# A layer of convolution by scan and a 4-bit feed-forward: statistics in sets of groups 0 to 3 and 4 to 7, the first x wholly through GpSimd, last banks opened by ScalarE, and new orders

## The reference

```
xn  = (x - mean) / sqrt(var + 1e-5)                    # over the last axis
out = x + conv(xn) + ffn(xn)

conv: a causal convolution along the sequence with the complex filter
      init * phazor^t, phazor = exp((angle*1j - exp(l)) * scale),
      plus last_conv * phazor^(t+1); times the gate 1 - exp(-exp(l)*scale); the real part
ffn:  q(v) = each block of 16 along the last axis divided by max|.|/6, rounded to the
      grid 0, .5, 1, 1.5, 2, 3, 4, 6 with its sign, and multiplied back
      gate = q(xn) @ q(w_gate).T;  up = q(xn) @ q(w_up).T           # 352 wide
      h = silu(gate) * up;         ffn = q(h) @ q(w_down).T         # 128 wide
```

## Time and profile before

| | |
|---|---|
| median of 3 runs | 121.2 us (119.83 to 121.43) |
| profiled execution | 120.77 us |
| its span, first to last instruction | 118.7 us |
| busy PE, DVE, ACT, POOL | 109.0, 101.6, 105.4, 100.3 us |
| granted TensorE clock | 1.00 |
| moved by DMA | 4.90 MB |

### The profile page before, as it was taken

How to read it: one execution, slowest core, us unless ns; L and a number is a source line. 1 busy time by engine, 2 the same in 40 slices (tenths; PEclk the granted TensorE clock), 3 DMA queues, 4 the chain that set the end, 5 groups by cost and what they waited for, 6 DMA issues and landing times.

```text
span 118.7 us, 2355 instructions
## 1 busy us (share of the span) xinstructions
PE 109.0 (92%) x661; PEld 83.6 (70%) x661; DVE 101.6 (86%) x219; ACT 105.4 (89%) x229; POOL 100.3 (85%) x119
## 2 busy tenths in 40 slices
PE   0599799989699999999999999999999999999992
PEld 0599455355357577877788876787788878879891
DVE  0798899999999999999899999898998699998300
ACT  4798889999999998999999999898989899898640
POOL 4578887991999999999999899999899999999400
DMA  3992000000000000020002000200020020020202
GB/s 98 340 359 104 0 3 0 3 3 6 0 0 0 0 0 0 0 94 0 0 3 94 0 3 0 88 0 6 0 88 0 0 88 0 6 91 0 88 22 66
DMA packets 3323, 4.90 MB, mean 41 GB/s; under 512 B 496, under 2 KB 1392, under 8 KB 3312
## 3 DMA queue, kind: packets, MB, share of 16 engines
q1 hardware_dynamic: 3168, 4.77, 11.6%
q10 hardware_dynamic: 144, 0.00, 0.1%
HBM read 2.67 MB, written 2.10 MB: 40 GB/s over the span
## 4 chain that ended last, share of the span: by engine, by line
PE 69%; ACT 12%; DVE 5%; issue 2%; ACTq 0%; DVEq 0%
PE ps_o L1305 16%; PE ps_u L1250 14%; PE ps_g L1231 14%; PE ps_h L1269 8%; PE ps_u L1257 6%; ACT xn L805 3%; PE ps_o L1294 3%; PE ps_x L1216 2%; PE ps_x L1202 2%; ACT silu L849 2%; ACT sqh L862 1%; ACT xsq L813 1%; DVE ps_u L1724 1%; DVE ps_u L1691 1%; ACT xq_T L842 1%
## 5 line engine op out<-in xcount | busy, mean ns | idle before, releaser
L1231 PE MATMUL ps_g<-wg_T,xq_T 128*128 128x352 f32 x64 | 25.0, 472 | 0.6 <-ACT silu L849 0.2
L1305 PEld LDWEIGHTS ps_o<-wd_T,hq_T 128*128 128x128 f32 x174 | 22.2, 192 | 2.1
L1305 PE MATMUL ps_o<-wd_T,hq_T 128*128 128x128 f32 x174 | 23.6, 275 | 0.0
L1250 PE MATMUL ps_u<-wu_T,xq_T 128*128 128x352 f32 x64 | 22.6, 466 | 0.2 <-DVE hq L1732 0.2
L855 ACT COPY hq_T<-ps_h 128x384 f32<-128x384 f32 x32 | 15.3, 479 | 2.8 <-PE ps_h L1269 2.8
L1685 DVE TENSOR_TENSOR ps_u<-silu,ps_u 128x704 f32<-128x704 f32 (+1 forms) x17 | 14.4, 844 | 2.2 <-PE ps_u L1250 2.1
L1269 PE MATMUL ps_h<-ident,hq 128*128 128x128 f32 x96 | 15.9, 274 | 0.3 <-ACT wd_T L782 0.2
L849 ACT ACTIVATE silu<-ps_g 128x352 f32<-128x352 f32 x32 | 14.9, 464 | 1.0 <-PE ps_g L1231 0.9
L1269 PEld LDWEIGHTS ps_h<-ident,hq 128*128 128x128 f32 x96 | 11.7, 142 | 5.1 <-issue 3.7
L1691 DVE TENSOR_REDUCE ps_u<-ps_u 128x44 f32<-128x704 f32 (+1 forms) x17 | 14.3, 849 | 0.2
L1724 DVE TENSOR_TENSOR ps_u<-ps_u,inv 128x704 f32<-128x704 f32 (+1 forms) x17 | 14.3, 845 | 0.2
(11 more groups left out here) (171 smaller groups left out, 246.1 us busy)
## 6 DMA issues: line engine op xcount, KB each, us to landing
x_all<-x_in SPq DMA_DIRECT2D x8, 256.0 KB, 4.6
out<-x_all SPq DMA_DIRECT2D x7, 256.0 KB, 2.0
w_raw<-w_in SPq DMA_DIRECT2D x2, 192.0 KB, 3.4
out<-x_all SPq DMA_DIRECT2D x4, 64.0 KB, 1.6
w_raw<-w_in SPq DMA_DIRECT2D x1, 176.0 KB, 3.6
par<-params_in ACTq DMA_DIRECT2D x1, 3.5 KB, 3.0
```

The source lines that it names most:

```text
L1231: pe.matmul(ps_g[:, 0:I], x_cols(t), wg_T[:, :], start=True, stop=True).then_inc(s_gate, 1)
L1250: pe.matmul(slot(q)[:, j, 0:I], x_cols(t), wu_T[:, :], start=True, stop=True).then_inc(s_up, 1)
L1305: m = pe.matmul(out_cols(t), hq_T[t % NHT][:, c * P:(c + 1) * P], wd_T[:, c, :], start=False, stop=(c == NCH - 1), skip_group_check=True)
```

## The change

The statistics now come in a set of groups 0 to 3 and a set of groups 4 to 7; the temporaries of the second lie in pair 3's slot, so its first step waits for up tile 7. Groups 2 and 3 are normalised from the first set. With `XH = 0`, both halves of group 0 go through `divide_x`, `square_x`, `big_x`, `shift_x`, `shift_back_x` and `scale_x`; `divide_first`, `square_first`, `round_first` and `scale_first` have no calls any more. A new step `open_last` (ACT) copies x of the last three tiles into their banks, and `sum_parts` waits for it in place of its own matmuls. Pair 9 instead of pair 12 is scaled on POOL. The first warm-up has 29 products instead of 21. And the four lists have new orders; SP's list of DMAs is the same. The definitions of `whole_turns` and `out_table` are only moved in the text.

```
-    STAT = ((0, 2), (2, 8))
-    STAT_SLOT = (0, 1)
-    XH = 1
+    STAT = ((0, 4), (4, 8))
+    STAT_SLOT = (0, 3)
+    XH = 0
-    BY_POOL = (11, 12, 13)
+    BY_POOL = (9, 11, 13)
...
+        s_openl = sem("x_in_last_banks")
...
-            return (ps_o[:, 0:D], slot(LAST - 1)[:, 0, 0:D], ps_x[:, 0:D], ps_g[:, 0:D])[t - (NT - TG)]
+            return (ps_o[:, 0:D], slot(LAST - 1)[:, 0, 0:D], ps_x[:, GT - D:GT], ps_g[:, 0:D])[t - (NT - TG)]
...
+            def open_last(t):
+                if t == NT - 3:
+                    slot_read(act, LAST - 1)
+                elif t == NT - 2:
+                    act.wait_ge(s_xnTc, NG)
+                else:
+                    act.wait_ge(s_silu, NT)
+                act.copy(last_bank(t), x_all[:, t, :]).then_inc(s_openl, 1)
...
                 else:
-                    if t == NT - 3:
-                        slot_read(pe, LAST - 1)
-                    elif t == NT - 2:
-                        pe.wait_ge(s_xnTc, NG)
-                    else:
-                        pe.wait_ge(s_silu, NT)
-                    pe.matmul(out_cols(t), ident[:, :], x_all[:, t, :], start=True, stop=True)
+                    pe.wait_ge(s_openl, t - (NT - TG))
```

More of the change, by code:

```diff
@@ L953, in _ @@
-            normalise(3, 1)
-            normalise(3, 2)
-            silu_tile(5)
-            normalise(3, 3)
-            square_h(1)
-            square_x(2, 1)
-            big_h(1)
-            big_x(2, 1)
-            copy_weight(2)
+            normalise(3, 3)
+            square_x(2, 1)
+            copy_xqT(1, 1)
+            big_x(2, 1)
+            square_h(1)
+            silu_tile(4)
+            big_h(1)
+            copy_in_table(1)
+            silu_tile(5)
+            out_table(0)
@@ L974, in _ @@
-            normalise(4, 1)
-            silu_tile(8)
-            big_x(3, 1)
-            normalise(4, 2)
-            copy_hT(2)
-            silu_tile(9)
-            normalise(4, 3)
-            copy_xnT(1)
-            square_h(3)
+            silu_tile(10)
+            copy_hT(2)
+            copy_xnT(1)
+            normalise(4, 0)
+            normalise(4, 1)
+            normalise(4, 2)
+            square_h(3)
+            normalise(4, 3)
+            big_h(3)
+            turn_part(0, 0)
@@ L1032, in _ @@
             big_h(7)
-            copy_xqT(5, 1)
-            copy_hT(10)
+            copy_hT(12)
+            copy_xnT(4)
+            silu_tile(19)
+            silu_tile(20)
+            copy_hT(13)
             normalise(7, 0)
-            turn_state(1, 1)
-            copy_xnT(4)
-            copy_hT(11)
-            silu_tile(18)
+            square_h(8)
+            big_h(8)
             square_x(6, 1)
+            copy_hT(14)
+            silu_tile(21)
             big_x(6, 1)
-            copy_hT(12)
@@ L1043, in _ @@
-            square_h(8)
-            silu_tile(19)
-            big_h(8)
-            copy_hT(13)
             normalise(7, 1)
-            silu_tile(20)
-            copy_hT(14)
+            copy_hT(15)
+            normalise(7, 2)
             copy_out(2)
-            silu_tile(21)
-            normalise(7, 2)
-            normalise(7, 3)
-            copy_hT(15)
+            silu_tile(22)
             open_out(3)
             copy_hT(16)
-            silu_tile(22)
+            normalise(7, 3)
@@ L1834, in _ @@
             moments(22)
+            maxima_x(1)
             moments(23)
+            scales_x(1)
+            inverses_x(1)
+            maxima_x(2)
+            scales_x(2)
+            inverses_x(2)
+            product(0)
+            maxima_h(0)
+            decay_column(0)
+            scales(0)
+            decay_column(1)
+            inverses(0)
+            divide_h(0)
+            product(1)
+            maxima_h(1)
+            scales(1)
+            inverses(1)
+            divide_h(1)
+            scale_h(0)
             moments(24)
```

652 lines of the change are left out of this document (321 added, 331 removed).

## The result

The changed kernel takes 120.83 us, median of 20 runs (120.50 to 121.66), against 120.70 for the kernel before beside it: a ratio of 1.005, interval 1.0026 to 1.0076. The ratio leaves out runs that took over 1.5% longer than the fastest of their kernel, four of the kernel before and none of the changed one, and without those four the kernel before has a median of 120.2. So the changed kernel is a little slower, by half a per cent, where 119.5 was forecast.

A forecast was written before the change was run, and what follows sets the result against it. PE was taken to set the pace from 39 us and to wait on other engines before. A lead of 0.75 plus 0.7 from the tail, 1.45 us off 120.77, gave 119.3 profiled, 119.5 on the median; range 117.2 to 121.8.

The forecast's parts named there:

- Start of the first gate tile: Gate tile 0 starts at 17.1 us against 15.07, 2.0 later, after more moments on DVE and scaling on POOL.
- First table product: in_table(0) moves ahead of all gate tiles, from 12.3 to 14.0 us while PE waits: 1.75 us leave the path.
- Statistics of the second set: Groups 4 to 7's statistics between products of pairs 2 and 3: off the path, shift at 40.1 us, added wait costs nothing.
- Lead at up tile 10 ... I take 0.75: PE's work ahead when it saturates: 0.9 us at up tile 10 (45.1 for 45.48), taken as 0.75; bounds 0 and 2.7.
- From 39 us on PE sets the pace: From 39.29 us PE is busy 20.63 of 20.71 us; an instruction's price there is its distance to the next.
- Tail: At the end, three PE openings of the last banks become ACT copies: net 0.7 us gained, bounds 0.2 and 0.9.
- Costed at nothing: Group 0's first half on PE, longer warm-up (end 11.9 us), pair exchange, POOL's order and SP's queue: no cost.
- Pair 9 for pair 12 ... bounds 0.4 either way: POOL scales pair 9 instead of 12, DVE takes one 0.8 us scaling near the end: no cost, 0.4 either way.
- Rival 1: The hole between 17 and 45 us closes further: lead 2.7, tail 0.7, 117.4 to 118.0 us; chance 0.25.
- Rival 2: DVE takes PE's place where PE is saturated; its 0.3 lag is passed on, only the tail left: 120.3 us; chance 0.12.
- rival 3: Second shift late, ACT stands at normalise(4,0) with square_h(3) behind it; three microseconds late give 122.3 us; chance 0.10.
- Rival 4: PE's clock falls to the lower level while it has little work, 14.0 to 17.1 us: 120.5 to 121.5 us; chance 0.05.

The follow-up runs named there:

- e4: Changed kernel with in_table(0) back behind up tile 3 and its copy behind square_h(0): 123.20 us, ratio 1.0246.
- e1: Changed kernel with the x maxima of groups 1 and 2 written to PSUM: 120.53 us, ratio 1.0023.
- e14: Changed kernel with x maxima in PSUM; ACT normalises groups 2 to 7 two tiles at a time, every second tile's statistics left out: 120.29 us, 0.9963.
- e11: Changed kernel with x maxima in PSUM; ACT normalises groups 5 to 7 two tiles at a time, second tile's statistics left out: 120.27 us, 0.9997.
- e6: Kernel before with the new tail up to up tile 11, then the remaining steps in the changed kernel's order: 122.12 us, ratio 1.0136.
- e3: Changed kernel with x maxima in PSUM; on ACT square_h(3) and big_h(3) moved ahead of most of group 4's normalised tiles: 121.15 us, 1.0060.
- e10: e8 with three more moves: moments(29 to 31) ahead of maxima_x(3), copy_hT(0) ahead of open_out(0), normalise(5, 1) behind big_h(4): 120.76 us, 1.0017.
- e7: Changed kernel with x maxima in PSUM; pairs 11, 12, 13 on GpSimd instead of 9, 11, 13: 123.81 us, ratio 1.0286.
- e8: Changed kernel with x maxima in PSUM; five moments moved into DVE's earlier waits, nothing left out: 120.61 us, ratio 1.0005.
- e12: Changed kernel with x maxima in PSUM; DVE's maxima of h from pair 4 on read half the columns: 120.50 us, ratio 1.0007.

## Why the prediction was wrong

**Start of the first gate tile: right in time, in part by luck.** It came at 17.24 us for 17.1. The terms that the prediction counts up to the rescale of group 0 add up to 15.2 us and not to its 14.9, and the rescale started at 14.53. What came late in its place was POOL: spread_rstd(1) stands ahead of the scaling in its list, and the prediction, which has that scaling follow the rescale and end at 15.8, gives it no cost. The scaling ended at 16.19. DVE's rescale, then POOL's two steps:

```profile
14.53 0.24 DVE L1654 SCALAR_TENSOR_TENSOR den<-ps_u,rstd 128x16 f32<-128x16 f32 x2
```

```profile
14.59 1.03 POOL L564 TENSOR_TENSOR xn<-x_all,rstd 128x512 f32<-128x512 f32 x1
15.58 0.61 POOL L499 TENSOR_TENSOR xv<-xt,den 128x256 f32<-128x256 f32 x1
```

**First table product: right.** in_table(0) ran from 12.73 to 14.5 us in PE's wait, and moving it back costs 2.4 us, with a wait of 0.68 that is the move's own (e4). The 16.39 us at which the prediction has the old cosine made is its start; it ended at 17.11, and nothing hangs on it.

**Statistics of the second set: right.** Their shift ended at 40.70 us (40.1), and normalise(4, 0) started at 40.90 straight behind ACT's copy, with no wait for it. The wait for up tile 7 cost nothing that shows.

**"Lead at up tile 10 ... I take 0.75": wrong.** Measured are -0.02 against the profiled execution of the kernel before, and -0.4 to -0.6 against the three other traces with its start. Two things failed. The first is the reference: the prediction took 45.48 us, from one execution whose warm-up had been long, for the kernel's up tile 10, where the three others have 44.88 to 45.09, so 0.4 to 0.6 of the 0.75 were never there to be won. The second is the walk through the four lists, which was late by 0.96 us at up tile 10 (46.06 for 45.1). Of these, 0.14 were there at gate tile 0; 0.35 are the stalls of the two x scales, removed by e1; 0.18 are left between gate tile 0 and up tile 8 (23.08 us for 22.9), not tied to one place by any run; and 0.29 lie between up tiles 8 and 10 (5.39 for 5.1). In that last stretch round_h(3) has an excess of 0.53 us with ACT's tiles of group 4 single and 0.13 in pairs (e14), but only 0.13 of what is saved reaches up tile 10; with DVE's and POOL's work cut as well, 0.35 does. The bound of 0 that the text gave for this term was the right end; its reason, that DVE's lag is passed on, is not what the runs show.

**"From 39 us on PE sets the pace": wrong, 0.82 us.** The same steps in another order were taken to run at the same pitch because PE showed 20.63 of 20.71 us busy. The old order left 0.73 us of excess between up tiles 10 and 30, the new one 1.42, in waits of 0.06 to 0.35 us, most of them under what the idle column shows: eleven of them in the new order, seven in the old. Relief of ACT's queue gives back 0.3 (e11). Reliefs on all three engines leave 0.91, still above the old order's 0.73 without any relief, so at least 0.2 is not reached by them. That it lies in how the steps are interleaved is likely (e6 agrees: the new order behind the old start has more excess too), but how the loss splits over single places is open, as each wait that was closed opened the next (e3, e10).

**Tail: right,** 0.63 us (and 0.5 alone) for 0.7; turn_h(30) did not wait, turn_h(29) did, 0.17.

**Costed at nothing.** PE's warm-up ended at 11.87 us (11.9). That number is luck: in the twelve other traces with the new start it ended between 11.34 and 12.68. That it costs nothing is not luck: gate tile 0 does not follow it there (17.27 us behind the latest end, 17.80 behind one at 11.50), while in the kernel before the warm-up holds DVE, as shown above. Of "Pair 9 for pair 12 ... bounds 0.4 either way" nothing is shown: going back in the new order, at the places tried, cost 3.3 us (e7), which is a matter of those places.

**Rivals.** Rival 1 did not happen. Rival 2 gave 120.3 us, but its mechanism was not borne out: DVE had over 1 us to give away before 30 us (e8) and 4 us later (e12), and PE took none. Of rival 3 a piece happened, ACT's tiles of group 4 ahead of square_h(3), not late but in the way (0.13 us at up tile 10, e14). Rival 4's time, 120.5 to 121.5, holds the measured 120.83, but by luck: its fall of the clock did not happen in the changed kernel (1.00 in every window). In one of four runs of e4, with in_table(0) no longer in that place, it did.

## What to carry to other kernels

Where several engines are over 95% busy, a full engine is not yet the bound: remove some of its work and see whether the next step moves, or only a wait appears. When an order is changed in such a stretch, compare pitches between landmarks, not busy shares: here 0.7 us was lost in waits most of which were too short for the idle column. Take the times of a reference from more than one trace: the same start differed by 0.6 us from one execution to another. And of a small VectorE step that is moved, ask what GpSimd is doing at its new place.

## What the runs showed of the hardware

- A scaling of 32 columns in SBUF on VectorE took 0.53 and 0.79 us beside GpSimd's elementwise steps and ended 0.03 and 0.04 us behind them; with its source in PSUM it took 0.17 and 0.19.
- How many of the warm-up's products are slow differs from run to run: 11 to 17 of 42 had a record of over 0.4 us in four traces of the old start (the block took 6.11 to 6.80 us), and 10 to 23 of 58 in thirteen of the new one (7.83 to 9.18 us); the others' records last about 0.28. Only the old start passed this on to its gate tile 0.
- TensorE's granted clock was 0.59 from 17.40 to 20.00 us in one of four runs of e4, so most of that stretch at the lower of its two levels, 1.2 of 2.4 GHz. From 12 to 15 us PE had been busy 1.00 of 3.00 us; from 20.00 on, behind 2.60 us without a pause, the rows give 1.00 again.
- Four ACT copies of 128 columns run 0.20 us apart, though each lasts 0.28.
